# Added bf16 products of a constant tile on TensorE in an eight-layer attention and MLP kernel

## The chip, the cores and the metric

The kernel runs on one core of one Trainium2 chip. The metric is the device time of one execution in microseconds (us). Three executions of the kernel before were timed. One further execution was profiled, and all rows of the trace in this text are of that one.

## The reference, cut to what matters

x has 64 sequences of 64 rows of 128 numbers, in fp32. Eight layers follow each other, each added to x; the first six take a layer norm of x first, the last two take x as it is.

```python
x = x + _L0_xattn_ref(_layernorm(x), ctx_1024, ...)      # 16 heads of 8, queries from x, rotary, keys and values from ctx
x = x + _L0_ffn_ref(_layernorm(x), ...)                  # an attention of its own, 16 heads, l2-normalised, then a product
x = x + _L1_xattn_ref(ctx_1024, _layernorm(x), ...)      # cross attention, latent side from x
x = x + _L1_ffn_ref(_layernorm(x), ...)                  # routing to 2 of 8 experts, silu(x w1) * (x w3), w2
x = x + _L2_xattn_ref(_layernorm(x), ctx_1024, ...)      # 8 heads of 64
x = x + _L2_ffn_ref(_layernorm(x), ...)                  # routing to 2 of 8 experts with a capacity, gelu MLP
x = x + _L3_xattn_ref(x, ctx_1024, ...)                  # self attention, layer norm, cross attention, layer norm, MLP
x = x + _L3_ffn_ref(x, ...)                              # shifted mix, sigmoid(x W_r) * (relu(x W_k)^2 W_v)
return x
```

Nothing that the change adds is read by any of this.

## The kernel before

x is kept in SBUF as X, 32 tiles of 128 rows (a tile is two sequences). Nearly all products are fp32, most of them 128x128 or 128x256. The program is a row of stages, each in a block of its own; a stage begins when all engines have ended the one before.

| stage | function | us of the trace |
| --- | --- | --- |
| load, and first stage: attention of layer 0 | `load_stage` (L257), `attention0_stage` (L304) | 0 to 241 |
| second: the l2-normalised attention and the keys of layer 1 | `key_attention0_stage` (L586) | 241 to 431 |
| third: attention of layer 1 | `attention1_stage` (L786) | 431 to 628 |
| fourth: first layer of experts | `mixture_stage` (L2151) | 628 to 911 |
| fifth: attention of layer 2 and routing, then experts | `attention2_mixture_stage` (L1058) | 911 to 1181, 1181 to 1311 |
| tail: layer 3 | `tail_stage` (L1695) | 1311 to 1622 |

In each stage every engine has a program of its own, written by hand: PE (TensorE), DVE (VectorE), ACT (ScalarE), POOL (GpSimd) and SP (the DMA issues). Each is a call of `pipeline(engine, n, steps)`: a list of pairs (lag, function). In round t it calls each function in the order of the list for tile t minus its lag, so the order of the list is the order of the instructions, and an instruction that waits holds all behind it on its engine. The waits are on semaphores: `done(e, sem, u)` waits until `sem` has counted tile u, `free(e, sem, u)` until a buffer's user of an earlier tile is through, `landed` for a DMA.

First stage. PE first waits for a table (`s_ones`), then goes tile by tile: `project(u)` (L505, the products at L511 and the three lines behind) multiplies the normalised tile and a tile of the context into pQ, `scores(half)` (L523) writes the scores of 8 heads into PSUM `a_S` in two halves, each a pair of fp32 products of 32 rows and 512 columns; the second half waits for VectorE's maximum over the first (L438). Exponents on ScalarE (L483), `scores_t` (L542 to L550), values, output.

Second stage. `transpose_x(u)` (L723 to L727) turns the normalised tile over into pA, for which it waits for VectorE (f_xn, L251) and for the reader of pA in the round before; `project(u)` is L729 to L734. The order on PE in a round is scores(0), project, output, scores(1), transpose_x, product_v.

Third stage. Before PE's first tile it waits for tables made with one GELU (a large ACTIVATE of Y, L927). `transpose_x` is L985 to L988, the scores are L1006 (a bf16 product that writes a mask) and L1009 on top of it.

Fifth stage, attention: PE's rounds are written out as a loop over t (L1550). VectorE computes the rows' places in the experts' regions (`r_put`, L1306), GpSimd writes the rows there (L1189). When all rows have landed, the experts begin: SP loads 256 rows (`a_rows`), PE transposes them (L1574), multiplies by the first weights (L1585, hidden in 4 parts), ScalarE applies the GELU (L1420), PE the second weights (L1596).

Tail. Layer 3 is computed in 48 steps q, each of two tiles: `order` is 6 steps of self attention, 10 pairs of a self and a cross step, 6 cross steps and then 16 MLP steps. GpSimd gathers the experts' rows for the coming self steps (L2683) until some 1455 us. One program serves all three kinds; `in_both(f)` runs f in attention steps, `in_mlp(f)` in MLP steps. In a round PE goes through

```python
pipeline(pe, N, [
    (L + 4, in_both(product_v)), (L + 6, in_mlp(product)), (L + 5, in_mlp(mixes)), (L, transpose_x),
    (L + 1, in_mlp(output)), (L + 2, in_both(first_rows)), (L + 3, in_both(transpose_p)),
    (L + 4, in_mlp(transpose_n)), (L + 1, in_both(scores)), (L, in_both(project)),
    (L, in_mlp(hidden))], straight=True)
```

`transpose_x` is L2013 to L2021, `project` L2023 to L2041 (queries and keys of two tiles into one PSUM bank pQ, L2034 and L2035), `scores` L2049, `first_rows` L2055, `transpose_p` L2061, `hidden` L2077, `output` L2084 and L2086, `transpose_n` L2094, `mixes` L2106 and L2109, `product` L2117. Several of them share PSUM banks; `take_turn(turn_q, q)` waits until the last reader of pQ (ScalarE's copy into `t_qk`, L1920, or the relu of the hidden product) is through. DVE reads pW, of which the trace speaks as `t_pO`, in its chain to the output (`t_o`, L1891).

## Time and profile before

| | |
| --- | --- |
| times of three executions | 1615.68, 1627.61, 1626.73 us; median 1626.73 |
| span of the profiled execution | 1621.9 us |
| PE busy with products | 1344.7 us, 83% |
| PE weight loads | 1032.2 us, 64% |
| VectorE | 1050.1 us, 65% |
| ScalarE | 853.5 us, 53% |
| GpSimd | 540.3 us, 33% |
| DMA | 112 MB, 69 GB/s on average |

The profiled execution's own time isn't among the three; beside its span of 1621.9 the median is 4.8 us longer. PE is busy most, but its busy time contains the time in which its clock is down: PEclk in a row is the granted clock of TensorE as a part of full speed, 1.00 for 2.4 GHz, 0.50 for 1.2 GHz. The sum over engines hides what matters for this change, so the rows further down are of single stages and of stretches of them.

### The profile page before, as it was taken

The numbers are of one execution on the slowest core, as the hardware profiler recorded it, in microseconds if no ns is written. First come the engines' busy times: TensorE is split into PE (matmuls) and PEld (weight loads), VectorE is DVE, ScalarE is ACT, GpSimd is POOL, SyncE is SP. The second block draws the span as 40 slices with busy tenths as digits, with TensorE's granted clock in tenths as the row PEclk, the third lists the DMA queues.
The fourth block names the chain that finished last, engine by engine and source line by source line (L and its number), as shares of the span: only waits on it lengthen the run. The fifth ranks groups of instructions, "written<-read, shape, count | busy, mean of one in ns | idle before, by whom it ended". The sixth has DMA issues, their size and how long they took to land. (4 is left out here: it accounts for less than half of the span.)

```text
span 1621.9 us, 43697 instructions
## 1 busy us (share of the span) xinstructions
PE 1344.7 (83%) x15232; PEld 1032.2 (64%) x15232; DVE 1050.1 (65%) x3243; ACT 853.5 (53%) x2251; POOL 540.3 (33%) x974
## 2 busy tenths in 40 slices
PE   6999988999499996568999599889379937778887
PEld 3677755655356665457999467667279936666666
DVE  4888847799699998623444477775512226889564
ACT  2666645678677774452222145445134437777465
POOL 4555411111121101770000375664700056662332
PEclk9999995799899997589999789999689977889598
DMA  4423310000000000146777312222123311110001
GB/s 130 162 102 110 111 66 5 14 16 17 14 2 1 0 1 24 51 148 198 204 206 205 90 43 62 67 80 77 45 79 116 97 48 37 39 32 21 1 14 40
DMA packets 101745, 112.34 MB, mean 69 GB/s; under 512 B 11456, under 2 KB 83136, under 8 KB 101440
## 3 DMA queue, kind: packets, MB, share of 16 engines
q1 hardware_dynamic: 73792, 83.75, 16.4%
q0 software_dynamic: 8192, 16.79, 3.7%
q10 hardware_dynamic: 19584, 9.44, 2.0%
q8 instruction: 110, 1.80, 0.5%
q14 instruction: 67, 0.55, 0.1%
HBM read 69.05 MB, written 40.89 MB: 68 GB/s over the span
## 5 line engine op out<-in xcount | busy, mean ns | idle before, releaser
L2614 PE MATMUL e_H<-e_xT,e_w_up 128*128 128x256 f32 x480 | 111.5, 382 | 0.0
L2510 ACT ACTIVATE e_silu<-e_H 128x256 f32<-128x256 f32 x120 | 42.6, 383 | 126.6 <-DVE e_y L2452 89.8
L483 ACT ACTIVATE a_PT<-a_ST 128x1024 f32<-128x1024 f32 x64 | 65.6, 1025 | 75.8 <-PE a_ST L550 75.8
L438 DVE TENSOR_REDUCE a_mx<-a_S 128x8 f32<-128x1024 f32 x64 | 78.2, 1221 | 31.3 <-PE a_S L523 31.1
L2614 PEld LDWEIGHTS e_H<-e_xT,e_w_up 128*128 128x128 f32 x480 | 89.1, 192 | 10.7
L2439 DVE TENSOR_TENSOR e_h<-e_silu,e_H 128x256 f32<-128x256 f32 x120 | 47.7, 420 | 57.6 <-ACT e_silu L2510 57.4
L1420 ACT ACTIVATE a_h<-a_SO,a_w_down 128x256 f32<-128x256 f32 x128 | 50.3, 475 | 65.6 <-PE a_SO L1585 63.3
L1336 DVE COPY a_rowsT<-a_pX 128x256 f32<-128x256 f32 x32 | 13.6, 425 | 108.5 <-PE a_pX L1574 108.5
L523 PE MATMUL a_S<-a_qkM,a_qk 32*128 32x512 f32 x256 | 77.8, 685 | 6.1 <-DVE a_mx L438 6.1
L1189 POOL DMA_INDIRECT slots_in<-R,r_put x64 | 63.2, 987 | 36.6 <-DVE r_put L1306 19.4
L1361 ACT ACTIVATE a_xT<-a_pQ 128x128 f32<-128x128 f32 (+1 forms) x44 | 14.3, 326 | 114.9 <-PE a_pQ L1450 82.4
L542 PE MATMUL a_ST<-a_qkM,a_qk 32*128 32x512 f32 x256 | 72.1, 640 | 1.4 <-ACT a_PT L483 1.4
L212 POOL MEMSET a_ln_half<- 128x1 f32 x3 | 0.3, 100 | 218.7 <-POOLq L2164 181.9
L2683 POOL DMA_INDIRECT Y<-slots_out,r_get x64 | 65.2, 1019 | 14.1 <-issue 13.9
L2683 POOL DMA_INDIRECT R<-slots_out,r_get x64 | 63.1, 985 | 19.5 <-issue 19.5
L1009 PE MATMUL a_S<-a_spread,a_blk 128*128 128x512 f32 x128 | 66.3, 600 | 0.0
L241 POOL TENSOR_TENSOR a_ln_rstd<-a_ln_moments,a_ln_half 128x1 f32<-128x1 f32 x96 | 19.6, 205 | 132.3 <-DVE a_ln_moments L235 131.6
L1596 PEld LDWEIGHTS a_pT<-a_w_down,a_h 128*128 128x128 f32 x512 | 62.1, 192 | 2.4 <-issue 0.8
L1585 PE MATMUL a_SO<-a_rowsT,a_w_up 128*128 128x256 f32 x256 | 63.2, 391 | 0.0
L1596 PE MATMUL a_pT<-a_w_down,a_h 128*128 128x128 f32 x512 | 62.4, 275 | 0.6 <-DVE a_y L1345 0.6
L2624 PEld LDWEIGHTS e_pY<-e_w_down,e_h 128*128 128x128 f32 x480 | 59.8, 192 | 2.8 <-issue 0.8
L2432 DVE COPY e_xT<-e_pX 128x256 f32<-128x256 f32 x40 | 17.0, 425 | 67.6 <-PE e_pX L2603 67.6
(433 smaller groups left out, 4195.2 us busy)
## 6 DMA issues: line engine op xcount, KB each, us to landing
slots_in<-Y SPq DMA_DIRECT2D x32, 512.0 KB, 3.4
e_w_up<-in_f_dram SPq DMA_DIRECT2D x40, 384.0 KB, 3.1
e_w_down<-in_f_dram SPq DMA_DIRECT2D x40, 192.0 KB, 2.9
e_rows<-slots_in SPq DMA_DIRECT2D x40, 128.0 KB, 2.8
slots_out<-e_y ACTq DMA_DIRECT2D x40, 128.0 KB, 2.7
keys_ahead<-e_keys SPq DMA_DIRECT2D x8, 512.0 KB, 3.2
a_k<-keys_ahead SPq DMA_DIRECT2D x8, 512.0 KB
a_rows<-slots_in SPq DMA_DIRECT2D x32, 128.0 KB, 2.1
```

The costliest lines, as they stand in the source:

```text
L438: nc.vector.tensor_reduce(mx[:, p % 2, 2 * half:2 * half + 2], S[:, :, :].rearrange("p g (h k) -> p g h k", k=D), AX, ALU.max).then_inc(s_ ...
L483: nc.scalar.activation(PT[:, p % 2, 2 * half:2 * half + 2].rearrange("p g h k -> p g (h k)"), ST[:, :, :], ACT.Exp, scale=SCALE).then_inc( ...
L523: i = nc.tensor.matmul(S[:, b, :], qk[r, p, 0, :], qkM[r, p, 1].rearrange("p h k -> p (h k)"), start=True, stop=True)
L542: nc.tensor.matmul(ST[:, b, :], qk[r, p, 1, :], qkM[r, p, 0].rearrange("p h k -> p (h k)"), start=True, stop=False)
L1009: nc.tensor.matmul(S[:, g, :], blk[:, p, g, :], spread[:, p, g].rearrange("p h t -> p (h t)"), start=False, stop=True).then_inc(s_S, 1)
L1189: nc.gpsimd.indirect_dma_start(xg[:, :], bass.IndirectOffsetOnAxis(ap=rt.put[:, kk, v:v + 1], axis=0), R[:, v, :], None).then_inc(s_put, 16)
L1420: i = nc.scalar.activation(h[:, p, hc, :], H[:, BANKS * p + b, CHUNK * c:CHUNK * (c + 1)], ACT.Gelu, bias=down[:, e % 2, HC * D + hc:HC * ...
L1585: i = nc.tensor.matmul(H[:, BANKS * p + b, CHUNK * c:CHUNK * (c + 1)], up[:, e % 2, lo:lo + P], rowsT[:, p, :], start=True, stop=True)
L1596: i = nc.tensor.matmul(pY[:, D * s:D * s + D], h[:, p, c, P * s:P * s + P], down[:, e % 2, D * c:D * (c + 1)], start=(c == 0), stop=(c == ...
L2614: i = nc.tensor.matmul(H[:, banks * p + b, CHUNK * c:CHUNK * (c + 1)], up[:, p, at:at + P], xT[:, p, :], start=True, stop=True)
L2624: i = nc.tensor.matmul(pY[:, D * s:D * s + D], h[:, p, c, P * s:P * s + P], down[:, p, D * c:D * (c + 1)], start=(c == 0), stop=(c == HC - 1))
L2683: net.nc.gpsimd.indirect_dma_start(t[:, u, :], None, rows, bass.IndirectOffsetOnAxis(ap=rt.get[:, k, u:u + 1], axis=0)).then_inc(rt.s_got[ ...
```

## The change

A bf16 tile `busy` of 128x512 is set to 1.0 by VectorE in the load stage. `keep_busy(net, out, n)` issues n products of it with itself on PE into a PSUM region `out` that is written by the next real product anyway, or by none. Nothing reads them. They stand

- in the load stage (9, into a new PSUM tensor);
- first stage: 10 of 384 columns ahead of PE's first wait, and 5 ahead of the projection of each of the first 8 tiles, where the wait for the reader of pQ (`s_sin`) now comes first;
- second stage: 12 at the start, 6 ahead of each of the first 8 `transpose_x`;
- third stage: 22 at the start, behind a new wait of PE for both GELUs (`s_g`), and 4 ahead of each of the first 6 `transpose_x`;
- fifth stage: 24 at the start, 6 in each of rounds 3 to 9, and 60 ahead of the experts behind a new wait until the last indices are written (`s_idx`);
- tail: 30 at the start, and in each of the 48 steps two pairs into pQ, one ahead of `first_rows` and one ahead of `project`, each behind `take_turn(turn_q, q)`.

The fourth stage is as before. PE has 513 products more, VectorE gains one memset in the load stage; the order of the other engines stays.

```diff
+def keep_busy(net, out, n):
+    for _ in range(n):
+        net.nc.tensor.matmul(out, net.busy[:, 0:P], net.busy[:, 0:out.shape[1]], start=True, stop=True)
...
 def load_stage(net):
+        @block.tensor
+        def _(pe):
+            pe.wait_ge(s_busy, 1)
+            keep_busy(net, unread[:, :], 9)
...
 def attention0_stage(net):
+            keep_busy(net, pY[:, D:512], 10)
             pe.wait_ge(s_ones, 3)
...
             def project(u, p):
+                free(pe, s_sin, u, bufs=1)
+                if isinstance(u, int) and u < 8:
+                    keep_busy(net, pQ[:, :, :].rearrange("p a t -> p (a t)"), 5)
                 done(pe, ln.s_xn, u)
                 landed(pe, s_cK, u, p % 2)
-                free(pe, s_sin, u, bufs=1)
...
 def key_attention0_stage(net):
+            keep_busy(net, pY[:, :], 12)
 
             def transpose_x(u, p):
+                if u < 8:
+                    keep_busy(net, pY[:, :], 6)
...
 def attention1_stage(net):
             def transpose_x(u, p):
+                if isinstance(u, int) and u < 6:
+                    keep_busy(net, pO[:, :], 4)
...
             pe.wait_ge(s_tb, 2)
+            pe.wait_ge(s_g, 2)
+            keep_busy(net, pO[:, :], 22)
...
 def attention2_mixture_stage(net):
+            keep_busy(net, pX[:, :], 24)
             for t in range(NT + 17):
+                if 3 <= t < 10:
+                    keep_busy(net, pX[:, :], 6)
...
+            pe.wait_ge(s_idx, NG)
+            keep_busy(net, pX[:, :], 60)
...
 def tail_stage(net):
+            keep_busy(net, pX[:, :], 30)
             pe.wait_ge(s_ones, 2)
...
+            def busy(n):
+                def step(q, _):
+                    take_turn(turn_q, q)
+                    keep_busy(net, pQ[:, :], n)
+                return step
...
             pipeline(pe, N, [
-                (L + 4, in_both(product_v)), (L + 6, in_mlp(product)), (L + 5, in_mlp(mixes)), (L, transpose_x),
-                (L + 1, in_mlp(output)), (L + 2, in_both(first_rows)), (L + 3, in_both(transpose_p)),
-                (L + 4, in_mlp(transpose_n)), (L + 1, in_both(scores)), (L, in_both(project)),
+                (L + 4, in_both(product_v)), (L + 6, in_mlp(product)), (L + 5, in_mlp(mixes)),
+                (L, transpose_x), (L + 1, in_mlp(output)), (L, busy(2)), (L + 2, in_both(first_rows)),
+                (L + 3, in_both(transpose_p)), (L + 4, in_mlp(transpose_n)), (L + 1, in_both(scores)),
+                (L, busy(2)), (L, in_both(project)),
                 (L, in_mlp(hidden))], straight=True)
```

PE in the second stage from its first instruction, before. The names in brackets are the semaphores that the instruction waits for: f0_xn is VectorE's normalised tile, f0_xt_out and f0_qkv are ScalarE's copies.

```order
L721 MATMUL f_pA<-W 128x128
L727 MATMUL f_pA<-W,f_xn 128x128 [waits f0_xn,f0_wowff_out]
L732 MATMUL f_pA<-f_xT,W 128x128 [waits f0_xt_out]
L733 MATMUL f_pA<-f_xT,W 128x128
L734 MATMUL f_pA<-W,f_xT 128x128
L727 MATMUL f_pA<-W,f_xn 128x128 [waits f0_qkv,f0_xt_out,f0_xn]
```

The same place after.

```order
L737 MATMUL f_pA<-W 128x128
L260 MATMUL f_pY<-busy 128x512 x12
L260 MATMUL f_pY<-busy 128x512 [waits f0_wowff_out]
L260 MATMUL f_pY<-busy 128x512 x5
L746 MATMUL f_pA<-W,f_xn 128x128 [waits f0_xn]
L751 MATMUL f_pA<-f_xT,W 128x128 [waits f0_xt_out]
L752 MATMUL f_pA<-f_xT,W 128x128
L753 MATMUL f_pA<-W,f_xT 128x128
L260 MATMUL f_pY<-busy 128x512 x6
L746 MATMUL f_pA<-W,f_xn 128x128 [waits f0_qkv,f0_xt_out,f0_xn]
```

Twelve products now stand ahead of the wait for f0_wowff_out and six behind it, and six between a projection and the next transpose.

PE in a cross step of the tail, before: t_pX is the transpose of the step's input, t_pS first the first rows, then the scores, t_pT the transposed probabilities, t_pQ queries and keys.

```order
L2021 MATMUL t_pX<-W,Y 128x128 x2
L2055 MATMUL t_pS<-t_count,W 128x2
L2061 MATMUL t_pT<-W,t_Pr 128x128 x2
L2049 MATMUL t_pS<-t_qk 64x64 x4
L2034 MATMUL t_pQ<-t_xT,W 128x256
L2035 MATMUL t_pQ<-t_cT,W 128x256
```

The same place after.

```order
L2056 MATMUL t_pX<-W,Y 128x128 x2
L260 MATMUL t_pQ<-busy 128x512 x2
L2090 MATMUL t_pS<-t_count,W 128x2
L2096 MATMUL t_pT<-W,t_Pr 128x128 x2
L2084 MATMUL t_pS<-t_qk 64x64 x4
L260 MATMUL t_pQ<-busy 128x512 x2
L2069 MATMUL t_pQ<-t_xT,W 128x256
L2070 MATMUL t_pQ<-t_cT,W 128x256
```

The first pair, which writes pQ, now has to wait for the reader of pQ ahead of first rows, transposes and scores; before, only the projection did.

PE in an MLP step of the tail, before: t_pRK are the mixes, t_pV the second MLP product and its bias, the last row is the hidden product.

```order
L2117 MATMUL t_pO<-W,t_k 128x128 x2
L2106 MATMUL t_pRK<-t_wr,t_sT 128x128 x4
L2109 MATMUL t_pRK<-t_sT,t_wk 128x256 x2
L2021 MATMUL t_pX<-W,Y 128x128 x2
L2084 MATMUL t_pV<-W,t_h 128x128
L2086 MATMUL t_pV<-W 128x128
L2084 MATMUL t_pV<-W,t_h 128x128
L2086 MATMUL t_pV<-W 128x128
L2094 MATMUL t_pT<-W,t_xs 128x128 x2
L2077 MATMUL t_pQ<-t_xT,W 128x256
```

The same place after.

```order
L2152 MATMUL t_pO<-W,t_k 128x128 x2
L2141 MATMUL t_pRK<-t_wr,t_sT 128x128 x4
L2144 MATMUL t_pRK<-t_sT,t_wk 128x256 x2
L2056 MATMUL t_pX<-W,Y 128x128 x2
L2119 MATMUL t_pV<-W,t_h 128x128
L2121 MATMUL t_pV<-W 128x128
L2119 MATMUL t_pV<-W,t_h 128x128
L2121 MATMUL t_pV<-W 128x128
L260 MATMUL t_pQ<-busy 128x512 x2
L2129 MATMUL t_pT<-W,t_xs 128x128 x2
L260 MATMUL t_pQ<-busy 128x512 x2
L2112 MATMUL t_pQ<-t_xT,W 128x256
```

One pair stands between the output product and the transposes, one between these and the hidden product; product, mixes and transposes of the input come first as before.

## Rows read from the trace of the kernel before

**Rows 1.** Table of windows, stages: length, busy time (instructions) per engine, clock, DMA.

```profile
core 0: us, PE busy (x) PEld busy (x) DVE busy (x) ACT busy (x) POOL busy (x), PEclk, DMA share, GB/s
431.00:628.00 197.00, 171.87 (x1854) 114.97 (x1855) 183.27 (x428) 149.35 (x406) 26.39 (x70) 0.95 0.00 1
...
1181.00:1311.00 130.00, 123.26 (x832) 115.03 (x832) 24.57 (x64) 51.63 (x129) 0.00 (x0) 0.96 0.32 93
...
1311.00:1496.00 185.00, 125.53 (x824) 102.98 (x824) 136.88 (x684) 123.38 (x342) 110.37 (x165) 0.80 0.14 35
```

**Rows 2.** Table of windows, stretches of the second stage.

```profile
243.70:307.70 64.00, 58.91 (x632) 34.75 (x632) 43.88 (x96) 34.95 (x100) 9.45 (x25) 0.50 0.02 7
264.80:273.80 9.00, 8.37 (x50) 4.32 (x46) 8.58 (x19) 5.76 (x15) 1.48 (x4) 0.50 0.01 2
279.03:301.29 22.26, 22.26 (x319) 13.57 (x315) 15.21 (x32) 13.24 (x45) 2.23 (x6) 0.50 0.03 8
331.70:341.60 9.90, 8.99 (x211) 5.76 (x211) 9.62 (x22) 7.86 (x30) 1.49 (x4) 1.00 0.06 17
```

**Rows 3.** Timeline, second stage: start, duration, line, tiles, [idle before, releaser].

```profile
244.91 0.44 PE L727 MATMUL f_pA<-W,f_xn 128*128 128x128 f32 x1 [3.23 <-DVE f_xn L251]
```

**Rows 4.** Table of windows, two stretches of two steps and one in the first stage.

```profile
18.73:33.74 15.01, 12.17 (x34) 5.63 (x33) 7.64 (x14) 4.47 (x11) 5.23 (x14) 1.00 0.05 13
...
53.34:59.52 6.18, 6.18 (x111) 4.45 (x110) 4.82 (x10) 3.96 (x8) 3.31 (x10) 1.00 0.30 109
```

**Rows 5.** Timeline of PE in the first stage.

```profile
10.95 0.64 PE L511 MATMUL a_pQ<-a_cK,W 128*128 128x128 f32 x2
...
41.64 0.70 PE L523 MATMUL a_S<-a_qkM,a_qk 32*128 32x512 f32 x2
...
44.18 0.70 PE L523 MATMUL a_S<-a_qkM,a_qk 32*128 32x512 f32 x2 [1.02 <-DVE a_mx L438]
...
46.44 0.39 PE L511 MATMUL a_pQ<-a_cK,W 128*128 128x128 f32 x2
```

**Rows 6.** Timeline of the third stage, from its start.

```profile
436.57 1.99 ACT L927 ACTIVATE Y<-Y 128x1024 f32<-128x1024 f32 x2
...
444.33 0.44 PE L988 MATMUL a_pXY<-W,a_xn 128*128 128x128 f32 x1 [14.74 <-DVE a_xn L251]
...
450.64 0.63 PE L1006 MATMUL a_S<-a_allow,a_identb 128*128 128x512 bf16 x1
451.07 1.06 PE L1009 MATMUL a_S<-a_spread,a_blk 128*128 128x512 f32 x2
...
452.61 0.38 PE L1006 MATMUL a_S<-a_allow,a_identb 128*128 128x512 bf16 x1
452.83 1.02 PE L1009 MATMUL a_S<-a_spread,a_blk 128*128 128x512 f32 x2
```

**Rows 7.** Timeline of the fifth stage where the experts begin.

```profile
1166.25 0.17 DVE L1306 CAST r_put<-a_dump 128x4 uint32<-128x4 f32 x1
...
1184.44 0.66 PE L1574 MATMUL a_pX<-W,a_rows 128*128 128x128 f32 x2 [20.54 <-DMA a_rows<-slots_in]
1186.23 3.62 PE L1585 MATMUL a_SO<-a_rowsT,a_w_up 128*128 128x256 f32 x8
```

**Rows 8.** Table of windows, cross steps and MLP steps of the tail.

```profile
1478.32:1486.09 7.77, 6.43 (x57) 5.27 (x53) 7.28 (x39) 5.82 (x17) 1.79 (x4) 1.00 0.12 36
1500.00:1524.29 24.29, 18.06 (x62) 13.03 (x61) 16.71 (x73) 10.60 (x28) 9.05 (x18) 0.57 0.01 1
1549.97:1557.47 7.50, 6.58 (x31) 5.40 (x31) 3.85 (x17) 3.90 (x11) 2.06 (x5) 0.77 0.00 1
1557.47:1563.31 5.84, 4.93 (x30) 3.91 (x31) 3.83 (x17) 3.90 (x11) 2.05 (x5) 1.00 0.28 90
```

**Rows 9.** Timeline of the tail, a cross step and an MLP step.

```profile
1480.78 0.60 ACT L1920 ACTIVATE t_qk<-t_pQ 128x512 f32<-128x512 f32 x1
1481.23 0.38 PE L2055 MATMUL t_pS<-t_count,W 128*128 128x2 f32 x2 [0.67 <-DVE t_nz L1823]
...
1557.47 0.68 PE L2117 MATMUL t_pO<-W,t_k 128*128 128x128 f32 x4 [0.92 <-DVE t_o L1891]
```

More of the change, by code:

```diff
@@ L2744, in build @@
                              for k in range(2 * (1 + IN_FLIGHT))]
+        net.busy = ctx.enter_context(nc.sbuf_tensor("busy", [P, 512], BF16))
         net.Y = ctx.enter_context(nc.sbuf_tensor("Y", [P, NT, D], F32))
```

6 lines of the change are left out of this document (4 added, 2 removed).

## The prediction

> **What bounds the kernel now.** I read the table of stages first, then stretches of a few microseconds, then the order of time where a number stood out. After the first stage the mean granted clock of TensorE (PE below) is 0.80 to 0.96 per stage, and no stage has one engine busy throughout but the experts, where it is PE (123 of 130 us) [rows 1].
>
> The second stage shows best what is lost. PE idles 3.23 us at its start [rows 3], the granted clock is at 0.50 from 243.7 to 307.7, 64 us, and stays there although PE is busy in nearly all of it. From 279.0 to 301.3 lie three tile steps of 7.42 us with PE never idle; from 331.7 to 341.6, at 1.00, two steps of 4.95, and those are VectorE's (9.62 busy of 9.90) [rows 2]. Half clock costs some 2.5 us per tile there.
>
> The first stage reads 1.00 from its start [rows 4], but its durations do not agree: a 128x128 fp32 product lasts 0.64 us at 10.95 and 0.39 at 46.44 [rows 5], the same ratio as that of the bf16 product in the third stage on either side of a rise of the clock (0.63, 0.38) [rows 6]. I take the durations: PE is at 1.2 GHz until about 41 us, and the column has merely no event before. Two steps take 15.0 us there; from 53 us a step takes 6.18 with PE never idle [rows 4], so what is won or lost ahead of it reaches the end.
>
> The price of an added product is its distance to the next one behind a bf16 128x512: 0.43 us at half clock, 0.22 at full [rows 6].
>
> **The change, part by part.** The added products write PSUM that nobody reads. Each costs issue time on PE, and each can keep or raise the clock.
>
> First stage. The 9 in the load stage (3.9 us) lie beside the loads for which all wait: nothing. The 10 of 384 columns take at most 3.2 us ahead of PE's first own product; 0.3 taken, 1.4 at most. With the clock up from there, the scores start 1.5 us sooner, no more, since GpSimd and the first table load of ScalarE hold them. Each of the next three steps becomes 2.54 us from first to second half of the scores (41.64 to 44.18, in which PE waits 1.02 for VectorE's maximum [rows 5]), 1.04 of scores, 1.08 of five added products, 0.89 of projection, 5.6 for 7.5: 5.7 won. The steps at 41.6 and 47.2 are at full clock already and get the five products too: 2.2 lost. -1.5-5.7+2.2+0.3, say **-5**. Ends: +2 (clock up only after 30 us), -8.
>
> Second stage. 18 products (3.9 us) ahead of the first transpose meet 3.23 of idle. The 6 ahead of each of the first 8 transposes (1.3 us) lie where PE waits for ScalarE or where VectorE sets the step (8.58 busy of 9.00 at half clock) [rows 2], so there little is won: 1.4 in the first three steps, 1.5 in the next two. Then the three steps of 7.42 and one of 7.0 become 4.9: 9.7. Two of 4.4 behind them, in which VectorE had less left to do, become 4.9: 1.0 back. Sum **-12** (-7 to -15).
>
> Third stage. PE now waits for the second GELU too (ScalarE's Y, two of them from 436.57, so 437.6; PE's first transpose is at 444.33 behind 14.74 us idle) [rows 6]. 26 products follow: 5.7 us at full clock, 11.2 at half; with a third of them cold 7.5, to 445.1, 0.8 late; four per step add some tenths, the scores win some back. VectorE sets this stage, so a late start is a late end: **+1** (-1.5 to +2.5).
>
> Fifth stage, attention. 30 products beside some 10 us of idle while GpSimd gathers; only three steps there are PE's at half clock: **-2.5** (0 to -4). Experts: the 60 products start at 1166.4, when the last indices are written, and take 13.0 us at full clock, 25.8 at half; with 12 cold 15.5, to 1182, against the first transpose of rows at 1184.44 behind 20.5 of idle [rows 7]. Saved is the half clock on the first hidden products (3.62 us for eight, half that at full) and on the second ones: **-3**; all cold, +9.
>
> Tail, gathers and mixed steps, to 1455: GpSimd's gathers and VectorE set the step with the clock at either level: **0** (-3 to +2).
>
> Tail, cross steps alone, to 1496: VectorE is busy 7.28 of 7.77 us in two steps [rows 8], PE idles 0.83 per step by its issue, 0.67 by its rows [rows 9]. Four products are 0.87 us. The first two also wait for ScalarE's copy of pQ (0.60 us from 1480.78), and behind them stands the first-rows product, now at 1481.23. PE's loop becomes 3.06+0.87 = 3.93 us against VectorE's 3.88; ten steps, **+0.6** (0 to +4).
>
> Tail, MLP steps: 5.84 us at full clock, in which PE waits 0.92 for VectorE's t_o [rows 9]; 7.5 where the clock is down for part (0.77) [rows 8]. Both pairs of products stand behind `output`, from which VectorE's chain to t_o starts, so 0.87 fits in the 0.92. If the clock stays up: 3.1 won from 1500 to 1524 (0.57, PE 18 busy of 24 us), 2.9 in the step of 8.8 behind it, 1.6 in each of four steps of 7.5, 1.0 in the last: 13.4. PE is then busy all of a step; in the cross steps, at 0.83, the clock stayed at 1.00 [rows 8]. I count 85%: **-11.5** (-4 to -13.4).
>
> Sum: -5-12+1-2.5-3+0+0.6-11.5 = -32.4. The profiled span is 1621.9; the median of the runs, 1626.7, leaves 4.8 around it if that execution was a usual one (the three runs spread over 12). Span 1589.5, time 1594.
>
> A rule against this: the Trainium skill, "TensorE: Matmul & The Clock Gate" (Part 1, the clock gate), says that "the ramp penalty is <1% of a typical kernel span". By it all parts together would win 16 us at most, time 1610 or more. The trace disagrees as to the extent: one stretch of 64 us at half clock is 4% of the span [rows 2].
>
> **The rivals.**
> A, the clock falls in the steps all the same. For: it fell within an MLP step with PE busy 6.58 of 7.50 us [rows 8]. Against: the added work fills the idle that is left. The MLP term is then no gain; four products at 0.43 in 0.92 of idle cost 0.8 on each of six cold steps, +5. -32.4+11.5+5 = -16, time 1611.
> B, half clock is hidden behind the other engines except where PE has no idle at all: only the four steps of the second stage pay, -9.7, time 1617. For: gathers, cross steps. Against: the MLP step of 7.5 beside that of 5.84. The page's rule would put the time near this one.
> C, slower: the turn that the added products take in the tail. They wait for the copy of pQ ahead of first-rows, transposes and scores, in 32 attention steps. With that wait (1.0 us from the end of the transposes to 1481.38) and 0.87 of products all in the loop, a step costs 1.87 more: +60, time 1654. It decides from 1.0 per step, 32 times, where it eats the 32.4. For: VectorE has 0.2 us per step to spare. Against: PE idles 0.83 there, more in mixed steps.
> D, the products never raise the clock and cost 0.43 each: +17 in the second stage, +13 in the first, +8 before the experts, +13 in MLP steps, +11 at other starts, time 1689. Against: the rise at 451 us came right behind bf16 128x512 and fp32 128x512 products [rows 6].
>
> **How the numbers follow.** Forecast 0.75 (own range 1580 to 1606), A 0.12, B 0.05, C 0.05, D 0.03. The good ends of all terms together give 1577; the range that leaves out 2 in 10 is 1578 to 1614, into A. A measurement can tell some 1% from no change, 16 us, so 1610.5 is the bound: faster are the forecast and half of A, 0.82; slower are C, D and some of the spread of B, 0.07; within it the rest, 0.11.
>
> **What would show it.** 128x128 products of 0.39 us before 20 us, and the third scores pair near 28 instead of 33.7; the clock at 1.00 all through the second stage, no step over 5 us, the stage 12 us shorter; the third stage's first transpose 1 us late; 3.7 us per chunk from the second expert chunk on; cross steps of 3.9; MLP steps of 5.85 with no wait for t_o left. Wrong would be a clock of 0.50 in those steps, PE waiting over 0.5 us for t_qk ahead of the products, or rows already there while the 60 still run.

## The result and the profile after

The change takes 1611.5 us (median of five executions, 1606.0 to 1615.8) against 1624.8 us before (median of five, 1615.68 to 1627.61). The ratio is 0.9928, interval 0.990 to 0.9955: 13 us or 0.7% faster, where 1594 was forecast and 16 us was named as the least that counts as faster. The profiled execution took 1609.6 us of span (before: 1621.9), so the two profiles differ by 12.3 us where the forecast's terms add up to 32.4. One execution of mlp_only took 1698.3 us at a mean granted clock of 0.808, where its other five read 0.919 to 0.929; it was in a slower state and is left out below.

First the table of windows of the changed kernel, for the stretches that answer to [rows 4], [rows 2] and [rows 8].

```profile
core 0: us, PE busy (x) PEld busy (x) DVE busy (x) ACT busy (x) POOL busy (x), PEclk, DMA share, GB/s
18.39:32.98 14.59, 11.75 (x43) 6.16 (x43) 7.64 (x14) 3.82 (x10) 6.53 (x18) 0.77 0.05 13
...
53.50:59.70 6.20, 6.20 (x112) 4.47 (x111) 4.15 (x9) 3.45 (x7) 2.89 (x8) 1.00 0.29 108
...
243.70:303.00 59.30, 54.33 (x794) 31.11 (x794) 46.79 (x106) 36.61 (x109) 11.62 (x31) 0.94 0.03 9
279.50:294.60 15.10, 14.72 (x316) 9.62 (x316) 14.52 (x32) 11.46 (x38) 2.22 (x6) 0.89 0.04 11
324.00:333.80 9.80, 8.96 (x211) 5.73 (x211) 9.53 (x21) 7.76 (x30) 1.48 (x4) 1.00 0.07 17
...
1469.20:1477.10 7.90, 7.77 (x62) 6.05 (x61) 7.40 (x41) 5.85 (x17) 1.78 (x4) 1.00 0.12 35
1497.00:1521.00 24.00, 18.43 (x70) 12.60 (x69) 16.39 (x72) 10.53 (x28) 9.03 (x18) 0.72 0.00 1
1542.73:1548.58 5.85, 5.75 (x35) 4.39 (x35) 3.96 (x17) 4.11 (x12) 2.06 (x5) 1.00 0.00 1
```

Read the clock column against that of before. In the second stage 0.50 over 64 us has become 0.94, and three steps that took 22.26 us take 15.1. In the tail the MLP steps from 1531 to 1584 us all take 5.85 us, and PE is busy 5.75 of them in the one shown. But two steps of the first stage still take 14.6 us (15.0 before), and the 24 us at the beginning of the MLP steps are as long as they were.

Where the 12.3 us came from is read by taking one instruction of VectorE near the end of each stage in both traces (VectorE's order is the same but for one memset) and subtracting. The rows of this table are all profiles of the study, the columns the stages; each number is the stage's length less that in the first profile of before. A figure in brackets marks a stage in which that kernel has none of the added products.

| profile | first | second | third | fourth | 5th, attention | experts | tail, attention | tail, MLP | all |
| --- | --- | --- | --- | --- | --- | --- | --- | --- | --- |
| forecast | -5 | -12 | +1 | 0 | -2.5 | -3 | +0.6 | -11.5 | -32.4 |
| the change | +2.5 | -10.3 | +3.1 | (-1.0) | +1.0 | -0.5 | +1.5 | -8.6 | -12.3 |
| change_again | +4.9 | -12.4 | +2.8 | (-0.2) | +1.1 | -0.4 | +1.3 | -8.4 | -11.2 |
| before_2 | (+0.5) | (+2.9) | (+0.8) | (-0.1) | (+5.2) | (-0.6) | (-0.2) | (-3.7) | +4.8 |
| before_3 | (+2.1) | (-2.4) | (+1.7) | (+0.5) | (-0.3) | (-1.4) | (-0.3) | (-2.6) | -2.8 |
| second_only | (+2.4) | +0.6 | (+1.8) | (-0.8) | (+0.2) | (-1.5) | (+0.7) | (-2.6) | +0.7 |
| second_longer_only | (+2.6) | -11.6 | (+1.7) | (-0.5) | (0.0) | (-0.1) | (+0.3) | (-3.7) | -11.3 |
| tail_only | (+2.4) | (-6.1) | (+2.6) | (-0.5) | (+1.2) | (-0.5) | +0.9 | -8.3 | -8.3 |
| first_start_only | +1.4 | +0.5 | +2.0 | (-0.6) | +0.9 | -0.6 | +1.3 | -8.5 | -3.6 |
| first_in_wait | +2.1 | -10.7 | +2.6 | (-0.2) | +1.0 | -0.3 | +1.7 | -8.6 | -12.4 |
| first_both | -5.0 | -11.4 | +2.9 | (-0.2) | +3.9 | -0.4 | +1.5 | -8.6 | -17.4 |
| second_longer2 | +2.1 | -10.5 | +2.1 | (-0.2) | +1.1 | -0.4 | +1.7 | -8.6 | -12.7 |
| second_32_rows | +2.4 | +9.7 | +2.4 | (-0.6) | +1.1 | -0.5 | +3.4 | -9.0 | +8.8 |
| fifth_edits | +2.6 | -12.3 | +3.1 | (-0.6) | (+1.6) | -2.8 | 0.0 | -8.5 | -17.0 |
| mlp_only | +2.7 | -10.7 | +3.1 | (-0.1) | +1.0 | -0.5 | -0.2 | -10.4 | -15.2 |
| mlp_more | +0.7 | -12.3 | +2.6 | (-0.1) | +1.2 | -0.4 | -0.1 | -10.6 | -19.0 |
| best | -4.4 | -10.4 | (+2.8) | (+2.0) | (+2.3) | -2.8 | +2.5 | -8.5 | -16.5 |

Against the forecast, 7.5 us are missing in the first stage, 3.5 in the fifth stage's attention, 2.5 ahead of the experts, 3 in the MLP steps. The table also shows what one profile is worth: the bracketed numbers are stages without added products, and they differ by up to 9 us. In the tail's attention steps mlp_only, mlp_more and best have the 30 products at the start, but no pairs.

### The profile page after: what moved, and what is told of

Its sections match the earlier page's. It is cut to its first block and busy times, and to the rows that moved or that the text cites. A ratio compares the mean times of both kernels' runs of the same rounds, so it can differ in the third digit from the quotient of the medians.

```text
span 1609.6 us, 44724 instructions
## 1 busy us (share of the span) xinstructions
PE 1402.4 (87%) x15745; PEld 1043.4 (65%) x15745; DVE 1050.5 (65%) x3244; ACT 854.2 (53%) x2251; POOL 539.5 (34%) x974
## 5 line engine op out<-in xcount | busy, mean ns | idle before, releaser
L2650 PEld LDWEIGHTS e_H<-e_xT,e_w_up 128*128 128x128 f32 x480 | 89.2, 193 | 10.7
L260 PE MATMUL t_pQ<-busy 128*128 128x512 bf16 x192 | 62.0, 409 | 21.6 <-ACT t_qk L1948 20.8
L539 PE MATMUL a_S<-a_qkM,a_qk 32*128 32x512 f32 x256 | 72.7, 643 | 6.2 <-DVE a_mx L451 6.2
```

Source lines behind the costliest of these rows:

```text
L260: net.nc.tensor.matmul(out, net.busy[:, 0:P], net.busy[:, 0:out.shape[1]], start=True, stop=True)
L539: i = nc.tensor.matmul(S[:, b, :], qk[r, p, 0, :], qkM[r, p, 1].rearrange("p h k -> p (h k)"), start=True, stop=True)
L2650: i = nc.tensor.matmul(H[:, banks * p + b, CHUNK * c:CHUNK * (c + 1)], up[:, p, at:at + P], xT[:, p, :], start=True, stop=True)
```

## The experiments

The runs were made in four groups, on three chips. Each group had executions of the kernel before beside it, and every ratio is against those of its own group. second_only, second_longer_only and tail_only are the kernel before with products in one place; they also keep VectorE's memset and the earlier place of the wait `s_sin` in the first stage.

### The first stage: what the five products per step do

At 18.4 us the changed kernel is at full clock, as forecast. This is PE's timeline from there.

```profile
20.94 1.13 PE L539 MATMUL a_S<-a_qkM,a_qk 32*128 32x512 f32 x4 [1.42 <-DVE a_mx L451]
22.00 1.96 PE L260 MATMUL a_pQ<-busy 128*128 128x512 bf16 x5
23.75 0.63 PE L526 MATMUL a_pQ<-a_xn,W 128*128 128x128 f32 x2
...
28.23 1.14 PE L539 MATMUL a_S<-a_qkM,a_qk 32*128 32x512 f32 x4 [1.42 <-DVE a_mx L451]
29.30 2.31 PE L260 MATMUL a_pQ<-busy 128*128 128x512 bf16 x5
31.41 0.63 PE L526 MATMUL a_pQ<-a_xn,W 128*128 128x128 f32 x2
```

PE waits 1.42 us for the maximum, the scores run at full clock (1.13 for four), and the clock falls: the projection's products take 0.63 again, not 0.39. The five added products are then paid mostly at half clock, 1.96 and 2.31 us where 1.08 was counted. Two stretches of the same kernel, one on either side of the first fall, show it in the column of the clock.

```profile
19.00:22.40 3.40, 1.98 (x10) 0.54 (x7) 2.39 (x6) 1.51 (x4) 1.44 (x2) 1.00 0.07 19
22.40:25.80 3.40, 3.40 (x14) 2.46 (x14) 1.02 (x2) 0.19 (x1) 1.82 (x7) 0.50 0.00 0
```

PE was busy 1.98 of 3.4 us before it fell, and all of the 3.4 us behind. The products stand behind the gap that costs the clock, not in it.

**first_start_only** takes the five away and leaves the 19 at the start.

```diff
-                if isinstance(u, int) and u < 8:
-                    keep_busy(net, pQ[:, :, :].rearrange("p a t -> p (a t)"), 5)
```

> The change without the five products ahead of each of the first 8 projections of the first stage; the 9 and 10 at the start stay. In the change the steps at 20 to 40 us still took 7.2 to 7.6 us although they began at full clock, because the clock fell three times (22.4, 29.2, 36.0 us) while PE waited for the maximum, and the five products then ran at 0.43 us each. Theory 1, the five cost what they win: without them those steps take 5.1 to 5.6 us while the clock is up and 7.5 where it is down, and the steps behind 40 us are 1.1 us shorter each; first stage at 60 us is 1 to 3 us earlier than in the change. Theory 2, without them the clock stays at half until 42 us as before: steps of 7.5, at 60 us the same 0.9 us late or later.

Measured: one execution, 1620.12 us. The clock came up at 7.2 us, fell at 10.6 and stayed down until 44.7: the window 10.60 to 44.70 reads 0.50 with PE busy 27.58 of 34.10. At 60 us the kernel was 1.4 us behind the first profile of before, the change 0.9. (At the stage's end the change is the later one, since its clock fell once more at 227 us.) Theory 2. The five products do buy the clock for about half of the time from 20 to 40 us, but no time that these profiles can show: at 60 us the seven kernels that have them in this form are 0.5 to 4.9 us behind the first profile of before (mean 1.9), the six without any product in this stage 0 to 2.6 (mean 1.7). The 4.9 is the change itself, profiled again: its clock was down from 20.1 to 30.3 us at a stretch.

**first_in_wait** puts the products into the wait for the maximum instead: five of 384 columns ahead of each half of the scores, for the first five tiles.

```diff
             def project(u, p):
                 free(pe, s_sin, u, bufs=1)
-                if isinstance(u, int) and u < 8:
-                    keep_busy(net, pQ[:, :, :].rearrange("p a t -> p (a t)"), 5)
...
             def scores(half):
...
                 def fn(u, p):
                     done(pe, s_msk, u)
+                    if isinstance(u, int) and u < 5:
+                        keep_busy(net, pY[:, D:512], 5)
```

> The change with the five products of the first stage taken from ahead of the projection and put into PE's wait for VectorE's maximum instead: five of 384 columns ahead of each half of the scores, for the first 5 tiles. Theory 1, the clock fell because PE idled 1.42 us per half there: it now stays at 1.00 from 5.3 us on, three steps take 5.1 to 5.6 us instead of 7.2 to 7.6, and the first stage ends 5 to 7 us earlier than in the change. Theory 2, the falls come from something else (the loads, products of 32 rows): falls at half a step's distance remain, and the products add up to 4 us.

Measured: one execution, 1611.48 us. The clock fell at 12.0 us, among the first projections, where nothing filled PE's waits any more, and came back at 29.0; from there it stayed up until 227 us. At 60 us the kernel was 0.5 us behind the first profile of before. Neither theory in full: the wait for the maximum was one of two gaps.

**first_both** fills both: it is first_in_wait with this added in `project`.

```diff
+                if isinstance(u, int) and u < 3:
+                    keep_busy(net, pQ[:, :, :].rearrange("p a t -> p (a t)"), 5)
```

> The change with the first stage's products in both places where PE idles: five ahead of each of the first 3 projections, and five of 384 columns in the wait for the maximum of each half of the scores, for the first 5 tiles (40 more products in all than in the wait alone; none ahead of the projections of tiles 3 to 7). With those of the wait alone the clock fell at 12.0 us and came back at 29.0. Theory 1, with both gaps filled it stays up from 5.3 us, the steps to 42 us take 5.1 to 5.6 us, and the first stage ends 4 to 7 us earlier than in the change; median 1605 to 1608. Theory 2, the steps are set by the other engines or by the loads: less than 2 us.

Measured: median 1606.74 us of ten executions (1599.93 to 1618.82), ratio 0.9922, interval 0.9892 to 0.9952. Its windows and its timeline in the first stage:

```profile
12.00:42.00 30.00, 26.80 (x168) 14.30 (x173) 18.79 (x40) 12.46 (x27) 17.06 (x44) 1.00 0.56 182
```

```profile
19.75 0.99 PE L260 MATMUL a_pY<-busy 128*128 128x384 bf16 x5
21.14 1.13 PE L541 MATMUL a_S<-a_qkM,a_qk 32*128 32x512 f32 x4 [0.41 <-DVE a_mx L451]
22.20 0.49 PE L526 MATMUL a_pQ<-a_xn,W 128*128 128x128 f32 x2
...
26.55 1.13 PE L541 MATMUL a_S<-a_qkM,a_qk 32*128 32x512 f32 x4 [0.41 <-DVE a_mx L451]
27.61 0.49 PE L526 MATMUL a_pQ<-a_xn,W 128*128 128x128 f32 x2
```

The five products take 0.99 us of the 1.42, 0.41 are left, and a step takes 5.41 us (21.14 to 26.55) instead of 7.3. The clock doesn't fall once in the stage; at 60 us the kernel is 5.0 us ahead of the first profile of before, 5.9 ahead of the change. best, with the same first stage, has no fall there either and is 4.4 ahead. This is the forecast's -5, by steps near the forecast's 5.6, with the products in another place. The times alone say less: change_again, in the same group of runs, has ratio 0.9947 (0.9915 to 0.9978), and the two intervals overlap.

### The second stage: what its products need to be, and for how long

**second_only** is the kernel before with this stage's products alone.

```diff
+            keep_busy(net, pY[:, :], 12)
...
+                if u < 8:
+                    keep_busy(net, pY[:, :], 6)
```

> The kernel before, with the added products of the second stage alone (12 at its start, 6 ahead of each of its first 8 transposes). In the full change this stage became 10.3 us shorter (from 2.5 us late to 7.8 us early). Theory 1, the gain belongs to this stage's own products and doesn't lean on what runs ahead of it: clock at 1.00 from some 248 us on but for single short falls, the stage 10 us shorter, median 1615, ratio 0.9935 to 0.995. Theory 2, it needs the products of the stage ahead (the clock must come up before): less than 5 us, ratio above 0.997.

Measured: median 1621.67 us of ten executions, ratio 0.999, interval 0.9959 to 1.0021. The ratio is that of theory 2, the mechanism that of neither: the products do bring the clock up from 247 us, without any help from ahead. The last of them ends at 274.6 us, and at 281.2 the clock falls.

```profile
247.30:281.20 33.90, 29.72 (x342) 15.79 (x340) 24.43 (x55) 19.73 (x52) 5.91 (x16) 1.00 0.01 3
281.20:315.30 34.10, 34.10 (x456) 21.08 (x452) 23.70 (x50) 19.62 (x63) 3.69 (x10) 0.50 0.03 9
```

The first window runs from the rise of the clock to its fall (1.00, PE busy 29.72 of 33.90 us), the second is what follows: 0.50 for 34.1 us while PE is never idle. It is the stretch of [rows 2] with its steps of 7.4 us, only later. The same fall came in first_start_only (280.2 to 314.4). In the change's first profile it lasted 3.4 us (281.8 to 285.2), in first_both 6.9 (from 269.8, where its products end at 265.5), and in change_again and the four others with these products it didn't come. Why it is long in two profiles and short or absent in seven is not shown.

**second_longer2** is the change with the products carried on into the stage's first ten outputs.

```diff
-                if u < 8:
+                if u < 9:
                     keep_busy(net, pY[:, :], 6)
...
             def output(u, p):
                 landed(pe, s_cX, u, p)
+                if u < 10:
+                    keep_busy(net, pY[:, :], 3)
```

> The change, and in the second stage six products also ahead of the ninth transpose and three ahead of each of the first ten outputs. Profiled with products for 8 transposes only, the clock fell at 280 to 282 us, where they end, and in two kernels stayed at half for 34 us with PE busy all the time. Theory 1, wide bf16 products are what brings and keeps the clock there: no fall lasts over 7 us, the stage takes as long as in the best case (10 us shorter than before), median 2 to 5 us under that of the change. Theory 2, the fall has nothing to do with the end of the products: falls of 34 us remain, and 30 products of 0.22 us add up to 6 us where PE has no idle.

Measured: median 1611.88 us of ten executions, ratio 0.9947, interval 0.9921 to 0.9973. No fall there, and VectorE is busy 33.15 of the same 34.1 us:

```profile
281.20:315.30 34.10, 33.73 (x739) 20.98 (x748) 33.15 (x70) 28.09 (x97) 5.20 (x14) 1.00 0.06 17
```

Against the change (change_again 1613.8, ratio 0.9947 as well) the median can't be told apart, and neither of the change's two profiles has the long fall. So the same edit was made on the kernel before: **second_longer_only** has the products of the second stage alone, in this longer form.

> The kernel before with the products of the second stage alone, but in the longer form (nine transposes, and three ahead of each of the first ten outputs). second_only, where they end at the eighth transpose, had ratio 0.999 and a fall of 34 us. Theory 1, the fall at the end of the products took the gain: with the longer form no fall over 7 us, stage 9 to 12 us shorter than in the first profile of before, ratio 0.993 to 0.996. Theory 2, the gain of this stage is lost elsewhere or isn't there in most executions: ratio 0.997 or more with a profile that shows the stage short.

Measured: median 1615.09 us of ten executions, ratio 0.9958, interval 0.9929 to 0.9987, against 0.999 for second_only; the stage 11.6 us shorter and no fall. The same stretch as in second_only, with PE again busy in all of it:

```profile
281.20:315.30 34.10, 34.10 (x752) 20.79 (x751) 33.13 (x71) 28.13 (x99) 4.98 (x14) 1.00 0.06 17
```

Theory 1, by the profiles: with products in it the stretch stays at full clock and the stage is 12 us shorter than in second_only. The two intervals of the ratios overlap, and second_only was profiled once, so it is not shown that all its executions have the fall.

**second_32_rows** keeps number, length and place of the change's products in this stage and takes them over 32 rows.

```diff
+            def keep_busy_32(n):
+                for _ in range(n):
+                    nc.tensor.matmul(pY[:, :], net.busy[0:32, 0:P], net.busy[0:32, :], start=True, stop=True)
-            keep_busy(net, pY[:, :], 12)
+            keep_busy_32(12)
...
-                    keep_busy(net, pY[:, :], 6)
+                    keep_busy_32(6)
```

> The change, with its 60 products of the second stage taken over 32 rows of the constant tile instead of 128: the same number, 512 columns and place. In two kernels PE stood at half clock for 34 us in this stage while it was busy in all of them. Theory 1, idle time alone lets the clock fall, so what fills it doesn't matter: clock up from some 248 us as in the change, stage 10 us shorter than before. Theory 2, products over few rows count for little: the clock stays at half from the start of the stage as before (243 to 293 or 308 us), and 60 products at 0.43 us make the stage up to 10 us longer than in the change or more.

Measured: one execution, 1632.56 us, the stage 9.7 us longer than before and 20 longer than in the change.

```profile
246.50:304.60 58.10, 57.37 (x363) 26.79 (x360) 30.06 (x66) 22.32 (x58) 6.88 (x19) 0.50 0.01 3
```

PE is busy 57.37 of 58.10 us and stays at 1.2 GHz, where the change is at 1.00 from 247.7 to 281.8. Theory 2. One profile, but the difference is far beyond what unaltered stages show: the added products work by what they are, and not only because they fill idle time.

### The fifth stage

In the changed kernel's timeline the 60 products end before the rows are there:

```profile
1161.89 15.05 PE L260 MATMUL a_pX<-busy 128*128 128x512 bf16 x60 [2.67 <-DVE r_put L1329]
...
1179.64 0.69 PE L1602 MATMUL a_pX<-W,a_rows 128*128 128x128 f32 x2 [2.69 <-DMA a_rows<-slots_in]
...
1181.46 3.62 PE L1613 MATMUL a_SO<-a_rowsT,a_w_up 128*128 128x256 f32 x8
```

The first hidden products take the same 3.62 us as in [rows 7]: the clock that the 60 had brought up by 1166 is gone after 2.69 us of idle. **fifth_edits** makes them 72 and takes the products out of the stage's attention.

```diff
-            keep_busy(net, pX[:, :], 24)
...
-                if 3 <= t < 10:
-                    keep_busy(net, pX[:, :], 6)
...
-            keep_busy(net, pX[:, :], 60)
+            keep_busy(net, pX[:, :], 72)
```

> The change with two edits in the fifth stage, read apart: no products in its attention part (24 at the start, 6 in each of rounds 3 to 9), and 72 instead of 60 ahead of the experts. In the profiles with the attention's products that part lost 0.9 to 1.1 us, without them 0.2 or won 0.3. Ahead of the experts the 60 ended at 1176.9, PE idled 2.7 us until the rows had landed and the clock fell at 1179.5. Theory 1: attention part 1 us shorter than in the change; the 72 reach the rows, the clock stays up, and from the first transpose of rows to the end of the experts it takes 2 to 3 us less. Theory 2: the clock falls there whatever stands ahead, or the first hidden products aren't on the path: less than 0.5 us, or up to 1 us later because the 72 run into the rows.

Measured: one execution, 1606.73 us.

```profile
1160.97 17.46 PE L260 MATMUL a_pX<-busy 128*128 128x512 bf16 x72 [2.67 <-DVE r_put L1329]
...
1178.74 0.44 PE L1599 MATMUL a_pX<-W,a_rows 128*128 128x128 f32 x2 [0.31 <-DMA a_rows<-slots_in]
...
1180.10 1.89 PE L1610 MATMUL a_SO<-a_rowsT,a_w_up 128*128 128x256 f32 x8
```

Now 0.31 us of idle, 1.89 us for the eight products, and the experts 2.8 us shorter than in the first profile (0.5 in the change). Theory 1, and it is the forecast's -3; best has the same -2.8, against a mean of -0.7 in the six profiles without products there. In the attention part the change's 1 us of loss in the first rounds is gone (at 950 us VectorE is 0.2 late, 1.0 to 1.2 in all nine profiles with the products). Its total of +1.6 arises from 1130 to 1150 us, where the clock fell once more (1130.4 to 1133.8), far behind the products; before_2 (+5.2), without them, and first_both (+3.9), with them, have such falls too. How the loss may arise is read in the change: six products from 938.03 to 940.75 at half clock, 2.72 us, ahead of the first full round. It isn't proved by that, since best, without these products, is 0.9 late at the same place.

### The tail

**tail_only** is the kernel before with the tail's products.

```diff
+            keep_busy(net, pX[:, :], 30)
...
+                (L, transpose_x), (L + 1, in_mlp(output)), (L, busy(2)), (L + 2, in_both(first_rows)),
...
+                (L, busy(2)), (L, in_both(project)),
```

> The kernel before, with the added products of the tail alone (30 at its start, two pairs in each of 48 steps). In the full change the attention steps lost 1.6 us and the MLP steps won 8.9. Theory 1: the same here, 7.3 us in all, span near 1614.5, median 1617 to 1618, ratio 0.995 to 0.997, MLP steps of 5.85 us. Theory 2, the 30 at the start and earlier stages decide it: MLP steps of 7.5 us remain in part, ratio above 0.998.

Measured: median 1616.88 us of ten executions, ratio 0.9956, interval 0.9928 to 0.9983; MLP steps of 5.85, tail as in the change. Theory 1. (Its span was 1 us below the expectation's: the second stage, untouched, was 6.1 us shorter, the first and third 5.0 longer together.)

**mlp_only** keeps the pairs to the MLP steps.

```diff
                 def step(q, _):
-                    take_turn(turn_q, q)
-                    keep_busy(net, pQ[:, :], n)
+                    if order[q][0] == "m":
+                        take_turn(turn_q, q)
+                        keep_busy(net, pQ[:, :], n)
```

> The change with the two pairs per step in the tail's 16 MLP steps only; the 32 attention steps have none. Theory 1, all of the tail's gain (8.6 us in the four profiles with the pairs) is in the MLP steps, and in the attention steps they cost some 1 us: attention steps 0.5 to 1.5 us shorter than in the change, MLP steps the same 5.85 us, median 1 us under the change's or not to be told from it. Theory 2, the pairs in the cross steps keep the clock up into the MLP steps: without them it falls at the beginning of these and the MLP steps lose 2 to 4 us.

Measured: median 1609.49 us of five executions (1606.48 to 1619.98; ratio 0.9958, interval 0.9921 to 0.9995), too few and too scattered to tell it from the change. In its profile the attention steps are 1.7 us shorter and the MLP steps 1.8 us shorter than in the change. Theory 1 for the attention steps, with a reservation: fifth_edits has the change's tail, pairs and all, and its attention steps are at 0.0, while best, without the pairs, is at +2.5. Theory 2 is excluded by this profile. The extra 1.8 us at the beginning of the MLP steps was in no expectation; it came again in mlp_more (-10.6) and not in best (-8.5), so it may hang on where the falls come. What the pairs did in the attention steps is shown by the waits of PE from 1305 to 1495 us (time, times, longest), in the change first, then in mlp_only.

```profile
PE t_pQ L260 <- ACT t_qk L1948: 20.8, 13, 2.1
PE t_pQ L2069 <- ACT t_xT L1966: 11.6, 8, 3.2
```

```profile
PE t_pQ L2070 <- ACT t_xT L1966: 24.3, 14, 4.9
PE t_pS L2091 <- DVE t_nz L1851: 18.4, 18, 1.9
PE t_pX L2057 <- ACT R L1693: 7.9, 1, 7.9
```

PE waits for the copy of pQ, as rival C had it, but the wait takes the place of that for t_nz and of half of that for t_xT (32.4 us in all against 42.7) and isn't added to them. The wait for R, 7.9 us, is in both.

**mlp_more** is mlp_only with seven products ahead of the hidden product of the first four MLP steps.

```diff
-                        keep_busy(net, pQ[:, :], n)
+                        keep_busy(net, pQ[:, :], max(n, at_first) if order[q][1] < 4 else n)
...
-                (L, busy(2)), (L, in_both(project)),
+                (L, busy(2, 7)), (L, in_both(project)),
```

> As mlp_only, with 7 instead of 2 products ahead of the hidden product of the first four MLP steps, where PE then waits 0.8 to 2.8 us for ScalarE. In mlp_only the MLP part won 10.4 us, in the change 8.6; the forecast was 11.5, all of it 13.4. Theory 1, the falls at 1494 and 1504 us come from that idle time: they go, and the MLP part wins 11.5 to 13. Theory 2, the products delay the hidden product on the path by 1.1 us a step: nothing or 2 us lost against mlp_only.

Measured: one execution, 1604.83 us. The clock reads 1.00 from 1489 to 1507 us, so the falls go as theory 1 says, but the MLP part wins 10.6 us against 10.4: those first steps hardly get shorter with the clock up. What sets them is not shown.

### All together, and the scatter

**best** combines first_both, the longer form in the second stage, no products in the third stage and the fifth stage's attention, 72 ahead of the experts, and pairs in MLP steps only; its edits are those shown.

> All that the runs so far favour: the first stage's products in both gaps, the second stage's also at the first outputs, none in the third stage and in the fifth stage's attention, 72 ahead of the experts, and the tail's pairs in MLP steps only. Against the change: first stage 6 us, second 0 to 4 (falls of 34 us gone), third 0.4, fifth attention 1, experts 0 to 2.5, attention steps 1.5, MLP steps 2: 11 to 17 us, median 1597 to 1602, ratio to before 0.981 to 0.987. Rival, the gains stand in each other's way through the phase of the clock's falls, and half of it is left: median 1603 to 1606.

Measured: median 1602.39 us of six executions (1600.53 to 1607.24), ratio 0.987, interval 0.9839 to 0.990: it is faster than the kernel before by 1.3%. The change's interval, 0.990 to 0.9955, begins where this one ends, and change_again's 0.9915 to 0.9978 lies above it; the two kernels never ran in one group. The median lies between the first theory's range and the rival's: 9 to 11 us under the change's medians, where 11 to 17 were added up. The profile is of its slowest execution.

**change_again** and **before_2**, **before_3** are the two kernels unaltered.

> The change once more, unaltered, for its scatter: how often is a stretch of the second stage at half clock, as in two of the four kernels profiled with its products (281 to 315 us), and not in the other two? Theory 1, the outcome of an execution hangs on where single falls of the clock come, some 8 us in the second stage alone: times scatter over 10 us or more (1603 to 1618), median near 1611, whatever the profile. Theory 2, the change is steady and only other edits moved the fall: times within 4 us.

> The kernel before, profiled a second time. Theory 1, its stages themselves vary with the clock's falls: the second stage differs by 2 to 8 us from the first profile, the MLP steps by 1 to 4 us (second_only, which has none of the tail's products, was 2.6 us shorter there), the third stage is 2 us longer, as in every other profile. Theory 2, its profile repeats within 1 us in each stage.

> The kernel before, profiled a third time; expectations as for before_2. If theory 1 holds, the mean of the three is what the gains of the stages must be counted from: second stage then 8 to 10 us won instead of 10 to 12, MLP steps 6 to 8 instead of 8.6.

Measured: change_again has median 1613.8 us of ten executions, 1606.51 to 1619.3, ratio 0.9947, interval 0.9915 to 0.9978. The kernel before ran from 1611.29 to 1631.77 us beside the first four experiments. before_2 had a span of 1626.7 us, before_3 1619.1. Where the second stage had no products, the clock came back at 308 (first profile), 316, 303 and 293 us (tail_only), and the stage's length follows it over 9 us. Theory 1 in the main: change_again's times lie 13 us apart, though its profile shows no fall in the second stage at all; the unaltered kernel's stages differ by up to 5.2 us from the first profile, and its third stage is 0.8 and 1.7 us longer, not 2.

## Why the prediction was right or wrong

The mean of the profiles without products in a stage is a better base than the first alone: first stage +1.7 (0, +0.5, +2.1, +2.4, +2.4, +2.6), second -1.4 (0, +2.9, -2.4, -6.1), third +1.6, MLP steps -2.5 (0, -3.7, -2.6, -2.6, -3.7).

- **The clock as the cause.** Right. Every gain is a stretch in which PEclk went from 0.50 to 1.00, and the first stage is at 1.2 GHz until some 42 us although the column of before reads 1.00: the changed kernel's column, which has events from 5 us on, reads 0.50 where a 128x128 fp32 product (x2 in the rows) takes 0.63 us.
- **First stage, -5: came +2.5 in the profile and +4.9 in change_again, 0.8 and 3.2 us slower than the mean without.** The failed step is "with the clock up from there ... each of the next three steps becomes ... 5.6 for 7.5". The clock was up at 5.3 us, and PE then waited 1.42 us per step for the maximum; the clock fell three times and the five products, priced at full clock (1.08 us), took 1.96 to 2.31. The steps took 7.3. first_both, with the products inside the waits, has steps of 5.4 and the stage 5.0 shorter.
- **Second stage, -12: came -10.3, -12.4 once more, 9 to 11 against the mean without, but only where the clock holds after the last product.** Step by step right: 18 products delay the first transpose, the first eight steps win little, the three steps of 7.42 become 5.0 on average. Not foreseen: the fall at 281 us, some 7 us behind the last product, 34 us long in two of the nine profiles that have them for 8 transposes, and in none of the three longer ones (the change's profile had 3.4 us of it). It accounts for second_only's profile (+0.6 in this stage), and so probably for its 0.999.
- **Third stage, +1: came +3.1, 1.5 more than the mean without (the ten profiles with products have 2.7 on average, the seven without 1.6, so 1.1 between them).** Right. GELU to first transpose is 8.63 us now, 7.76 before: 0.87 late where 0.8 was worked out. The changed kernel's timeline has the second GELU, the 26 products, 7.60 us of them where 7.5 were counted, and the transpose:

```profile
430.48 1.99 ACT L946 ACTIVATE Y<-Y 128x1024 f32<-128x1024 f32 x2
...
431.67 7.60 PE L260 MATMUL a_pO<-busy 128*128 128x512 bf16 x26 [8.15 <-ACT Y L946]
439.11 0.27 PE L1009 MATMUL a_pXY<-W,a_xn 128*128 128x128 f32 x1
```

- **Fifth stage's attention, -2.5: came +1.0.** The failed step is "only three steps there are PE's at half clock", for which 2.5 us were counted as won. The clock was indeed at 1.00 from 909.9 to 937.2 us, where before it was at 0.50 from 911.9 to 946.1, and up to 945 us VectorE's instructions came no more than 0.1 us sooner. From 950 on they are 1.0 late: six of the products stand in front of the first full round at half clock, and -2.5 had no part of this in it. That these are the 1.0 us is the likely cause, not a proved one.
- **Ahead of the experts, -3: came -0.5.** Failed step: "to 1182, against the first transpose at 1184.44". The span between the last product and the first rows, 2.4 us on paper and 2.69 measured, was taken as a margin, and it was what lost the clock. With 12 more products the -3 is there (-2.8).
- **Tail's attention steps, 0 and +0.6: came +1.5**, with best's +2.5 left aside 1.5 above the mean of those without the pairs; fifth_edits, with them, has 0.0. The forecast named PE waiting over 0.5 us for t_qk ahead of the products as a sign of being wrong: it came, 20.8 us in 13 waits, and yet the steps lost 1.5 us in all. The size was somewhat low: about half of the loss is there by 1380 us, in steps that were counted at 0.
- **MLP steps, -11.5: came -8.6 in the profile and -8.3 to -9.0 in eight others, 6 against the mean without.** Steps of 5.85 with no wait for t_o up to 1584 us, as forecast. The missing 3 us lie in the first 24 us: 3.1 were counted there for a clock at 1.00, it read 0.72, and the stretch got no shorter. But the clock isn't the whole of it, since mlp_more, at full clock in most of them, wins only 2 us more.

Rival A gives 1611, which is the time measured, but not by its mechanism: the clock holds in the MLP steps. That its number fits is chance. Rival B, half clock hidden except where PE has no idle, describes the fifth stage's attention and the beginning of the MLP steps; it isn't the whole, for the MLP steps won. Rival C decided nothing (1.5 us, not 60). Rival D was shown in one place, by an edit and not by the change: second_32_rows, where the products didn't raise the clock, cost 9.7 us in that stage, against the 17 that D had for it.

Behind all of it stands one way of counting that was wrong: the sum treated the clock as won for good once products stand ahead of a stretch. It was lost again in the next gap, or some us behind the last product, and the forecast had the numbers for three such places (1.02 in [rows 5], the end of the products at the eighth step, 2.4 us ahead of the rows). The range held the time, at its slow end; of the chances, 0.82 for faster than 1610.5 was too sure. Two slips in the forecast's own numbers change little: the good ends of its terms add up to -47.9, which gives 1579 and not 1577, and C and D alone have 0.08 where slower was given 0.07.

The forecast took from the Trainium skill, "TensorE: Matmul & The Clock Gate" (Part 1, the clock gate), that "the ramp penalty is <1% of a typical kernel span", and made of it that all parts together would win 16 us at most. The change's 13 us agree with that; best is 1.3% (1.0 to 1.6%) under the kernel before, 22 us by the medians of its runs (1602.39, 1624.39), and so just above it. The forecast's objection, one stretch of 64 us being 4% of the span, compared unlike things: the length of a stretch at half clock isn't its cost, and doing away with nearly all of this one shortened the stage by 9 to 12 us. The page's sentence is about the rise of the clock; here it rose and fell again many times in one execution.

## What to carry to other kernels

Products that only hold TensorE's clock belong inside its waits, the last one near to the end of the wait (0.31 us ahead held the clock here, 2.69 didn't); behind a gap that has cost the clock they are issue time at half clock. Look in each stage for what follows the last of them: in two of nine profiles the clock fell 6 to 7 us behind it, and although TensorE was then busy throughout, it took 34 us to come back. Before adding up gains of some us from one profile, take two or three of the unchanged kernel and look at how much its stages differ.

## What the runs showed of the hardware that was not expected

- TensorE can be busy without pause and stay at 1.2 GHz: 34.10 of 34.10 us in second_only, 57.37 of 58.10 in second_32_rows. The same 60 products over 128 rows brought the clock to 2.4 GHz within 4 us of the stage's start (244.3 to 247.7 in the change).
- In the experts' part the clock fell after 2.69 us of idle behind 60 products over all 128 rows, and held after 0.31 behind 72 (fifth_edits; 0.28 in best). In the first stage it fell after a wait of 1.42 us, in a stretch with PE busy 1.98 of 3.4.
- The same program differs by 20 us from execution to execution (1611.29 to 1631.77). Its three profiles lie 7.6 us apart (1619.1 to 1626.7), and the two largest differences go with the clock: in the second stage it comes back at 303, 308 or 316 us, and in before_2's fifth stage, 5.2 us longer, it falls twice more, at 1135.1 and 1145.3. That the whole 20 us come from this is not shown.
